# Edge chunks of two rows in place of four, in a sorted graph network kernel

## The reference

```
h = relu(layernorm(x))
# layer 1, four steps:
edge_mats = (edge_attr_16 @ W_bond + b_bond).reshape(-1, 32, 32)
msg = einsum('eij,ej->ei', edge_mats, h[dst])
agg = segment_sum(msg, src)
h = gru_cell(agg, h)
x = x + h
# layer 2:
g = relu(layernorm(x))
deg = segment_sum(1, dst);  d = where(deg > 0, rsqrt(deg), 0)
x = x + segment_sum(g[src] * (d[src] * edge_weight * d[dst]), dst)
```

## Time and profile before

| | us |
|---|---|
| median of three runs | 27753.59 (27752.26 to 27754.51) |
| the profiled execution | 27758.91 |
| its span | 27757.1 |
| block 1; its table clearing | to 732; to about 300 |
| sort, first to last row scatter | 882.8 to 4828.3 |
| a step, first to last gather | 4269.5 |
| end of a step's gathers to the next step's first | 181.6 |
| message scatters | 22846 to 27168 |
| POOL busy | 19766.5 (71%) |
| PE busy | 12374.2 (45%) |

### The profile page before, as it was taken

How to read it: one execution, slowest core, us unless ns; L and a number is a source line. 1 busy time by engine, 2 the same in 40 slices (tenths; PEclk the granted TensorE clock), 3 DMA queues, 4 the chain that set the end, 5 groups by cost and what they waited for, 6 DMA issues and landing times. The chain is left out here.

```text
span 27757.1 us, 248614 instructions
## 1 busy us (share of the span) xinstructions
PE 12374.2 (45%) x67675; PEld 9367.5 (34%) x67676; DVE 9831.1 (35%) x17524; ACT 4931.9 (18%) x12149; POOL 19766.5 (71%) x20823
## 2 busy tenths in 40 slices
PE   5566665455555455555455555545555530000004
PEld 5344443333333333333333333333333320000004
DVE  9899998222222222222222222222222230000007
ACT  7333333111111111111111111111111110000004
POOL 0677777777777677777677777767777767777771
PEclk8777777777777677777677777767777765555555
DMA  4233332111111111111111111111111111121113
GB/s 168 84 94 94 94 94 79 30 29 28 28 28 29 26 29 28 28 29 28 26 28 28 28 29 28 27 27 28 29 28 28 28 33 45 44 46 44 44 42 90
DMA packets 1814377, 1246.48 MB, mean 45 GB/s; under 512 B 1182629, under 2 KB 1744754, under 8 KB 1789679
## 3 DMA queue, kind: packets, MB, share of 16 engines
q1 hardware_dynamic: 583936, 850.03, 10.1%
q0 software_dynamic: 666016, 324.92, 8.0%
q10 hardware_dynamic: 564300, 70.11, 1.7%
HBM read 957.69 MB, written 285.80 MB: 45 GB/s over the span
## 5 line engine op out<-in xcount | busy, mean ns | idle before, releaser
L1083 POOL DMA_INDIRECT h_rows<-h_table,rec x13680 | 12910.7, 944 | 4284.0 <-issue 4118.8
L1233 PE MATMUL outer<-a_masked,h_by_quarter 128*128 128x136 f32 x27360 | 5316.2, 370 | 8726.5 <-DVE h_by_quarter L1124 8726.5
L1233 PEld LDWEIGHTS outer<-a_masked,h_by_quarter 128*128 128x128 f32 x27360 | 5045.0, 272 | 9193.2 <-issue 9193.2
L1279 ACT COPY outer_sums<-outer 128x408 f32<-128x408 f32 x4560 | 2276.2, 499 | 14770.2 <-PE outer L1233 14271.9
L1124 DVE TENSOR_TENSOR h_by_quarter<-h_rows,gates 128x1920 f32<-128x1920 f32 x912 | 1964.6, 2154 | 7011.0 <-DMA h_rows<-h_table,rec 7011.0
L1510 POOL DMA_INDIRECT messages_by_bucket<-ms,ix x3420 | 3279.1, 959 | 1063.5 <-issue 1042.4
L855 POOL DMA_INDIRECT edges_by_node<-row,place x3125 | 2992.9, 958 | 952.8 <-issue 945.2
L1117 DVE TENSOR_TENSOR a_masked<-rec,gates 128x2040 f32<-128x2040 f32 x912 | 2071.0, 2271 | 4308.7 <-PE outer L1233 4288.1
L1209 PE MATMUL msg_psum<-outer_sums,w_bond_blocks 128*128 128x480 f32 x7752 | 3521.2, 601 | 0.0
L1209 PEld LDWEIGHTS msg_psum<-outer_sums,w_bond_blocks 128*128 128x128 f32 x7752 | 1583.2, 215 | 1400.5 <-issue 1400.5
L1492 PE MATMUL pgb<-ident_f,gsp_by_chunk_of_tile 128*120 128x128 f32 x228 | 61.6, 426 | 3848.1 <-DVE gsp_by_chunk_of_tile L1430 3848.1
(11 more groups left out here) (277 smaller groups left out, 12593.5 us busy)
## 6 DMA issues: line engine op xcount, KB each, us to landing
h_rows<-h_table,rec POOLq DMA_INDIRECT x13680, 2.4
key_row<-source_keys SPq DMA_DIRECT2D x125, 1600.0 KB
rec<-edges_by_node SPq DMA_DIRECT2D x1140, 157.5 KB, 2.2
low_key_row<-source_low_keys SPq DMA_DIRECT2D x126, 800.0 KB
carry_flags<-carry_flags SPq DMA_DIRECT2D x285, 240.0 KB
mr<-messages_by_bucket SPq DMA_DIRECT2D x220, 264.0 KB, 2.7
messages_by_bucket<-zeros SPq DMA_DIRECT2D x36, 1600.0 KB, 37.0
chunk_sums<-scan_t ACTq DMA_DIRECT2D x912, 60.0 KB
```

The costliest lines, as they stand in the source:

```text
L1083: pool.indirect_dma_start(out=hb[j][:, u, :], out_offset=None, in_=ht, in_offset=bass.IndirectOffsetOnAxis(ap=rec[j][:, u, W_DST:W_DST + 1 ...
L1233: last = pe.matmul(pt[(j * NB + g) % RING][:, at:at + KC], hq[j % 2][:, u, :, :].rearrange("p q d -> p (q d)"), am[j % 2][:, u, :, :].rear ...
L1279: act.copy(ts[b][:, :, at:at + w].rearrange("p k (u c) -> p u k c", c=CPT), pt[(j * NB + g) % RING][:, 0:GPB * KC].rearrange("p (u k c) -> ...
```

## The change

CH becomes 2, so CPT becomes 16 and the product of a tile has 272 columns for 136. A node's edges are rounded up to whole chunks of two: T3 = 3232 tiles for 3420. J3 becomes 16 and GI 2: a step has 202 iterations of 16 tiles in 101 groups; GW = 512. GPB becomes 1 (a bank holds one product of 272 columns), so NB = 16 banks to an iteration, WEIGH_AT = 8 and HALF = 8. `rec` and `h_rows` have 2 x GI = 4 buffers, as before. `weigh` has two parts. In the message stage the buffers go from 4 to 2. Chunks in memory go from 109,440 to 206,848. The tables' blocks are of TB = 128 chunks, four to a group as before. Of the 98 flag scatters, 49 stay ahead of the sort; 49 go to POOL in the block behind it, which ends with the wait for all.

```diff
-CH = 4
+CH = 2
-J3 = 15
-GI = 4
-DIV15 = 4370
+J3 = 16
+GI = 2
+TO_ITERATION = 4096
...
+    TB = 128
+    NTB = GW // TB
...
                 def _(pool):
-                    for h in range(HB):
-                        pool.indirect_dma_start(
+                    def clear_flags(columns):
+                        for h in columns:
+                            pool.indirect_dma_start(
...
+                    clear_flags(range(HB // 2))
...
                     pool.wait_ge(s_sc[1], 16 * J1 * (IT1 // 2))
-                    pool.wait_ge(s_flag, 16 * HB)
...
+                @block.gpsimd
+                def _(pool):
+                    for h in range(HB // 2, HB):
+                        pool.indirect_dma_start(
...
+                    pool.wait_ge(s_flag, 16 * HB)
...
-            GPB = 3
+            GPB = 1
...
-                rec = [sb(f"rec3_{j}", [P, J3, W3]) for j in range(GI)]
-                hb = [sb(f"h_rows{j}", [P, J3, D]) for j in range(GI)]
+                rec = [sb(f"rec3_{j}", [P, J3, W3]) for j in range(2 * GI)]
+                hb = [sb(f"h_rows{j}", [P, J3, D]) for j in range(2 * GI)]
...
                             for j in range(GI):
                                 if j + 1 < GI:
-                                    make_a(n0 + j + 1, ng, j + 1, (j + 1) % 2)
-                                spread_h(n0 + j, ng, j)
+                                    make_a(n0 + j + 1, b * GI + j + 1, i, (j + 1) % 2)
+                                spread_h(n0 + j, b * GI + j, i, j)
                             if b == 0 and not last:
-                                make_a(n0 + GI, ng + 1, 0, 0)
+                                make_a(n0 + GI, GI, i, 0)
...
-                                    if g == WEIGH_AT and j == 2 and past == 2:
+                                    if g == 1 and j == 1 and past == 2:
                                         turn_scan(ng - 2, b)
...
-                                    if j == 3 and g == 2 and past == 2:
+                                    if g == NB // 2 and j == 1 and past == 2:
                                         store(ng - 2, b, s * USES[b] + i - 1, g_ - 2)
```

More of the change, by code:

```diff
@@ L114, in gnn_program @@
     GW = GI * NT
+    TB = 128
+    NTB = GW // TB
+    assert GW % TB == 0 and NT % TB == 0 and GW <= 512
     USES = ((NGR + 1) // 2, NGR // 2)
     assert T3 * P < BIG and T2 * P < BIG and HB <= P and HB * D <= 7 * 512 and NGR % 2 == 1 and NRUN % 4 == 0
-    assert T3 * DIV15 < 1 << 24 and all(t * DIV15 >> 16 == t // J3 for t in range(T3))
+    assert T3 * TO_ITERATION < 1 << 24 and all(t * TO_ITERATION >> 16 == t // J3 for t in range(T3))
     r3 = nc.dram_tensor("edges_by_node", [T3 * P, W3], F32).ap()
@@ L970, in _ @@
                     steps_v[0] += ch.n
-            s_rec = [sem(f"rec3_loaded{j}") for j in range(GI)]
-            s_hg = [sem(f"h_gathered{j}") for j in range(GI)]
+            s_rec = [sem(f"rec3_loaded{j}") for j in range(2 * GI)]
+            s_hg = [sem(f"h_gathered{j}") for j in range(2 * GI)]
             s_fl = [sem(f"carry_flags_loaded{b}") for b in range(2)]
@@ L1014, in gnn_program @@
                 sc = [sb(f"scan{b}", [P, GW]) for b in range(2)]
-                sct = [sb(f"scan_t{b}", [P, GI, P]) for b in range(2)]
+                sct = [sb(f"scan_t{b}", [P, NTB, P]) for b in range(2)]
                 cr = sb("carries", [P, NQ - 1, D])
@@ L1075, in group @@
                             for j in range(GI):
-                                pool.wait_ge(s_rec[j], ng * 16 + 16)
+                                r = b * GI + j
+                                pool.wait_ge(s_rec[r], s * (16 * USES[b]) + i * 16 + 16)
                                 pool.wait_ge(s_hb, n0 + j + 1)
@@ L1216, in turn_scan @@
                             hold(pe)
-                            for t in range(GI):
-                                last = pe.transpose(px[0:NT, t, :], sc[b][:, t * NT:(t + 1) * NT], ident_f[:])
+                            for t in range(NTB):
+                                last = pe.transpose(px[0:TB, t, :], sc[b][:, t * TB:(t + 1) * TB], ident_f[:])
                             last.then_inc(s_tr, 1)
@@ L1333, in gnn_program @@
                 fx = [sb(f"fx{r}", [P, J3]) for r in range(GI)]
-                gl = [sb(f"gl{b}", [P, GI, P]) for b in range(2)]
+                gl = [sb(f"gl{b}", [P, NTB, P]) for b in range(2)]
                 fl = [sb(f"carry_flags7_{b}", [P, GW]) for b in range(2)]
@@ L1337, in gnn_program @@
                 gpm = sb("gsp_by_chunk_of_tile", [P, GI, NT])
-                gc = [sb(f"gc{b}", [P, GI, P]) for b in range(2)]
+                gc = [sb(f"gc{b}", [P, NTB, P]) for b in range(2)]
                 sv = sb("span_rows", [P, NQ, D])
@@ L1490, in spread @@
                         hold(pe)
-                        for j in range(GI):
-                            last = pe.transpose(pgb[0:NT, j, :], gpm[:, j, :], ident_f[:])
+                        gpm_blocks = gpm[:].rearrange("p j (b k) -> p (j b) k", k=TB)
+                        for j in range(NTB):
+                            last = pe.transpose(pgb[0:TB, j, :], gpm_blocks[:, j, :], ident_f[:])
                         last.then_inc(s_gtb, 1)
```

92 lines of the change are left out of this document (47 added, 45 removed).

## The result

The changed kernel takes **28,621 us** (median of four runs, 28,613 to 28,625) where the kernel before takes 27,754 (27,752 to 27,755): a ratio of **1.031 [1.029, 1.033]**, slower by 867 us. The forecast was 28,345, slower, with a range from 27,500 to 29,000. The profiled execution has a span of 28,622.6 us, 865.5 over that of before.

A forecast was written before the change was run, and what follows sets the result against it. POOL bounds the kernel before; after the change a closed POOL-DVE-PE loop with slow clock restarts would. Steps +824, tails +40, messages -238, flags -36 sum to +590: 28,345 us, range 27,500 to 29,000.

The forecast's parts named there:

- The currency: Steps and messages: fewer tiles, less time; 752 fewer gathers at 1.248 us save 939 us if POOL is never held.
- The pause ahead of even iterations: Steps: PE idles 7.4 us while DVE does make_a, then spread_h, whatever POOL does.
- The mid wait and the odd pause: Steps: POOL's wait at DMA 8 for PE's eighth tile binds in even iterations; PE then pauses 3.3 us before odd ones.
- The two restarts: Steps: both pauses let PE's clock fall; each slow restart adds 1.95 us, making a group 44.4 us.
- The rule on pauses: PE in the steps: a loop that pauses each round pays the slow clock restart each round, despite busier PE.
- Tails: Step ends: PE's longer last iteration and weighing add 10 us a step, +40 us.
- Messages: Message stage: 188 fewer scatters at 1.264 us save 238 us, counted in full.
- the cover that the forecast weighed: Message stage: DVE's preparation hides in the 20.2 us iteration between, with two buffers; failing that, at most some 800 us.
- Flags: Flag scatters: moving 49 behind the sort saves 57 us there, 21 come back in the next block; -36 us.
- one restart per group: Rival, steps: the 3.3 us pause leaves PE's clock up; 42.4 us a group, 27,570 us total; chance 14%.
- the bound on POOL: Rival, steps: POOL still sets the pace, 40 to 40.5 us a group, some 26,700 us total; chance 8%.
- the slower ACT: Rival, steps: ACT's copies at 499 ns, or a wait per tile, slow PE; +680, 29,030 us total; chance 11%.

The follow-up runs named there:

- e_swap: Changed kernel with DVE's spread_h of an iteration ahead of make_a of the next; 33,993 us, ratio 1.026 to the kernel before beside it, late-signal chip.
- e_nomid_swap: Changed kernel without POOL's wait ahead of DMA 9 and with spread_h ahead of make_a; 27,697 us, ratio 0.998 to the kernel before, normal chip.
- e_nomid_swap_fill: Changed kernel without the wait ahead of DMA 9, spread_h ahead of make_a, six unread TensorE products behind each iteration; 35,723 us, ratio 1.075, late-signal chip.
- e_ch4: Changed kernel with CH = 4, so the old tile width, new grouping kept; 33,468 us, ratio 1.010 to the kernel before, late-signal chip.
- e_nowait: Changed kernel without POOL's two waits for PE ahead of its gathers; 39,905 us, ratio 1.204 to the kernel before, late-signal chip.
- after_again: Changed kernel, nothing edited, on a late-signal chip; 34,851 us, ratio 1.050 to the kernel before beside it.

## Why the forecast was right, step by step

- **The currency holds, and is lost in the loop.** 752 gathers fell away at an unchanged price each; the steps still became longer, since POOL is held: right.
- **The pause ahead of even iterations**: 7.4 forecast, 7.17 measured (median). It is DVE's 4.68 and 2.29 in a row, as costed (4.7, 2.3). The 0.2 us from PE's end to DVE's start was misread: the earlier trace rows show 0.04 (12583.00 + 1.55 to 12584.59), and 0.04 is the median after the change. Without that order the pause went in `e_swap`; in `e_nomid_swap` it stayed as long, set by the gathers. So the pause is "whatever POOL does" in the changed kernel only; with the order gone, late gathers alone make one as long.
- **The mid wait and the odd pause**: forecast 3.3, measured 3.92. POOL starts 0.79 us behind the half (12562.03 + 6.98 = 12569.01 to 12569.80), not 0.3, for which no row was given; from there to PE's start it is 13.67, forecast 13.6. This 0.5 us per group is the term that was mis-sized: the forecast's group is 44.4 us, the measured mean 44.93. 396 x 0.53 = 210 us, which is the whole difference of 1036 and 824. The measured loop is, in means, 7.20 of pause, 5.70 for the first half, 14.45 from its end to the odd start and 17.58 for the odd iteration; the forecast with its restarts has 7.4, 5.65, 13.9 and 17.45. So the other three terms are within 0.2 us. The mid wait also holds POOL behind one in six odd halves, where the forecast had it never bind.
- **The two restarts**: forecast 1.95 us each. First halves take 5.45 and 6.05 us (medians), against 3.83 and 4.27 where PE had not been idle: 1.6 and 1.8 lost there. From PE's first to its last instruction an even iteration takes 16.24 us and an odd one 17.58 (means), 1.9 and 2.1 over the 14.3 and 15.5 that the forecast has at full clock. That they lie on the loop is seen without any edit: over the even iterations of the changed kernel, the time from PE's start to that of the odd one follows the length of the first half with a slope of 1.01 (correlation 0.99); in the quarter with the shortest halves they are 5.34 and 19.79 us, in the slowest twentieth 6.99 and 21.45. From the odd half to the next even start the slope is 0.96 (0.95). In `e_nomid_swap`, without the mid wait, the length of a group no longer follows the even half (slope -0.1, for 1.5 in the changed kernel). What the full clock alone would give in the normal condition, no run tells.
- **The rule on pauses.** In the changed kernel every first half, behind pauses of 7.2 and 3.9 us (medians), runs in part at the low level (mean granted clock 0.69 and 0.70), and halves with no idle time ahead of them are at the high one (1.0 in `e_nomid_swap_fill`). The Trainium skill, "TensorE: Matmul & The Clock Gate", section "HAM oscillation — how this bites in real kernels", says that a loop which pauses each round pays each round; the traces agree, at 1.6 to 1.8 us for each restart's first half. The higher mean clock of the profile (0.87 in a step's gathers, 0.73 before) goes with more work on PE, and both restarts stayed slow under it.
- **ACT**: 385 ns forecast and measured; it never sets PE's pace in the normal trace.
- **Tails** +40 forecast, +38 measured.
- **Messages**: -238 forecast, -190 measured. The count is right; the pace went from 1.2636 to 1.278 us a scatter, some 47 us in all. The excess is not spread: in every seventh iteration, 28 in all, the second scatter starts 1.4 us late without a semaphore wait (40 us), and 41 scatters, each beside DVE's copy of 128x512 in the spread of g (L1443), take 1.15 to 1.26 us in place of 0.96 (10 us). The rows of one late scatter, in the changed kernel and in `e_ch4`:

```profile
24038.22 0.96 POOL L1524 DMA_INDIRECT messages_by_bucket<-ms,ix  x1 [0.30 <-issue]
24040.90 0.95 POOL L1524 DMA_INDIRECT messages_by_bucket<-ms,ix  x1 [1.72 <-issue]
...
28669.82 0.96 POOL L1524 DMA_INDIRECT messages_by_bucket<-ms,ix  x1 [1.71 <-issue]
```

`e_ch4` has it in every seventh iteration too, at the old width, and the kernel before has none. So it comes with the new grouping and buffers, not with the width, and it isn't the cover that the forecast weighed, since no wait for landed scatters ends there. Its cause is open.
- **Flags**: the sort ends 57 us earlier (4828.3 to 4770.9), as forecast. The next block grew by 33 us, not 21. Three of the moved scatters are long beside DVE's layer norm, 9 us in all (two of them below; the third, at 4805.77, takes 5.31 us):

```profile
4793.26 0.97 POOL L946 DMA_INDIRECT carry_flags<-zrow,flag_at  x1 [0.30 <-issue]
...
4793.90 3.42 DVE L894 TENSOR_TENSOR ln_tmp<-x_nodes,mean 128x3136 f32<-128x3136 f32 x1
4794.54 3.63 POOL L946 DMA_INDIRECT carry_flags<-zrow,flag_at  x1 [0.30 <-issue]
4797.36 3.42 DVE L895 TENSOR_TENSOR agg_h_one<-ln_tmp 128x3136 f32<-128x3136 f32 x1
4798.48 3.15 POOL L946 DMA_INDIRECT carry_flags<-zrow,flag_at  x1 [0.30 <-issue]
4800.82 3.42 DVE L896 TENSOR_REDUCE var<-agg_h_one 128x98 f32<-128x3136 f32 x1
4801.94 0.97 POOL L946 DMA_INDIRECT carry_flags<-zrow,flag_at  x1 [0.30 <-issue]
```

The misses of the parts all point one way: 212 us in the steps, 48 in the messages, 12 in the flags and 6 elsewhere, less 2 in the tails, are the 276 us between the forecast and 28,621. The rivals: one restart per group is refuted by both halves; the bound on POOL and the slower ACT by the waits. The second, POOL at 39.95 us a group, was not reached by any run. Open stays how the 924 us divide between swap and wait in the normal condition.

## What to carry to other kernels

Fewer work items for the busiest engine gain only while the loop that ties it to its neighbours has slack; add up that closed loop, pauses and wake-up of TensorE included, before counting items. When the loop comes out over the engine's own pace, look first at the order of operations and at waits placed for the old sizes: here one of each were together worth 924 us, more than the change lost. And read the kernel before beside each run: with the chip in another condition it took 19% longer, and the price of an edit measured there can't be carried over.

## What the runs showed of the hardware that was not expected

- On three of the four chips of the experiments the same kernels ran 5.4 to 6.2 ms longer, and signals came late: ACT's copy starts up to 14.8 us behind the end of PE's product in the changed kernel and up to 21.4 where POOL isn't held at all, for at most 0.04 in the normal condition; a wait of DVE with releaser "remote" takes up to 41.9 us in `e_nowait`. In `after_again` 387 of ACT's 399 long pauses ended 2.5 to 3.0 us after the last indirect DMA of a row of POOL's; in the other runs fewer did. On a fourth chip nothing of it shows. Why, no run tells.
- There, taking POOL's waits away made the kernel slower by 5 ms, and ACT's lag behind PE rose from 11.3 to 42.0 ms. That the waits keep signals moving would fit, but isn't shown.
- A scatter of POOL that starts beside a DVE TENSOR_TENSOR over 128x3136 ends 0.85 us behind that operation (4797.32 to 4798.17, 4800.78 to 4801.63) and takes 3.2 to 3.6 us; beside a TENSOR_REDUCE of the same size it takes its 0.97. The third long one spans a TENSOR_TENSOR and the TENSOR_SCALAR behind it and ends 0.13 us behind the latter. The Trainium skill, "SBUF — State Buffer", section "SBUF: two separate sides", has DVE and GpSimd share one pair of ports under an exclusive lock, which DVE takes in some operations only; these rows agree. It was not weighed in the forecast of the flags.
- Products without use made a kernel faster by 867 us (34,851 to 33,984, in the late condition): the granted clock in the first halves behind them rose from 0.62 to 0.96.
- In the message stage the second scatter of every seventh iteration starts 1.4 us late with no wait, at both widths (28 times in the changed kernel, 30 in `e_ch4`), and not in the kernel before. Why, no run tells.
